# Low halves of the next weights in 32 pieces on GpSimd, gelu output rounded by ScalarE instead of VectorE

## The reference

```python
def new_gelu(x): ...                                  # tanh form
shared = new_gelu(xf @ Wfc_s + bfc_s) @ Wproj_s + bproj_s
probs = softmax(xf @ Wr); topk_p, topk_i = top_k(probs, 2)   # made to sum to 1
for e in range(8):                                    # routed experts
    h = new_gelu(xf @ Wfc[e] + bfc[e]) @ Wproj[e] + bproj[e]
    routed = routed + h * gate[:, e:e + 1]
return shared + routed
```

## Time and profile before

| what | before |
|---|---|
| median of 3 runs (lowest to highest) | 1134.1 us (1130.27 to 1138.52) |
| profiled execution, first to last instruction | 1131.3 us |
| PE busy | 982.5 us (87%) |
| DVE busy | 804.5 us (71%) |
| ACT busy | 374.5 us (33%) |
| POOL busy | 444.0 us (39%) |
| mean granted TensorE clock | 0.934 |

### The profile page before, as it was taken

How to read it: one execution, slowest core, us unless ns; L and a number is a source line. 1 busy time by engine, 2 the same in 40 slices (tenths; PEclk the granted TensorE clock), 3 DMA queues, 4 the chain that set the end, 5 groups by cost and what they waited for, 6 DMA issues and landing times.

```text
span 1131.3 us, 21584 instructions
## 1 busy us (share of the span) xinstructions
PE 982.5 (87%) x6889; PEld 910.7 (80%) x6890; DVE 804.5 (71%) x2317; ACT 374.5 (33%) x851; POOL 444.0 (39%) x496
## 2 busy tenths in 40 slices
PE   5777888999999999998888797979979799797996
PEld 3556678888888888887887797979979799797996
DVE  3467788888888888887664767676676766767664
ACT  2011234434444444433342232323323233232332
POOL 4142445332333333434222536372453624545232
PEclk9677699999999999999997898989989899898998
DMA  9200510001111110001115535354532536352232
GB/s 263 95 10 10 163 38 29 30 24 33 37 37 37 37 37 26 25 18 34 39 68 175 162 55 147 76 124 98 127 97 48 132 87 129 98 126 28 47 46 29
DMA packets 48163, 82.68 MB, mean 73 GB/s; under 512 B 6416, under 2 KB 30883, under 8 KB 48132
## 3 DMA queue, kind: packets, MB, share of 16 engines
q0 software_dynamic: 31056, 57.46, 21.4%
q1 hardware_dynamic: 17076, 24.84, 7.5%
HBM read 55.32 MB, written 26.96 MB: 73 GB/s over the span
## 4 chain that ended last, share of the span: by engine, by line
PE 48%; issue 24%; DVE 15%; POOL 9%; ACT 1%; DMA 1%; SPq 1%; POOLq 0%; DVEq 0%; ACTq 0%
PE ps_nd L660 18%; PE ps_proj L645 9%; PE ps_ri L645 5%; PE ps_proj L725 4%; PE ps_ip L645 4%; DVE rden L1254 3%; POOL out L603 2%; PE ps_nd L846 2%; POOL v_rows L497 2%; PE ps_h L833 2%; POOL h L560 1%; DVE GL L1077 1%; PE ps_t L895 1%; PE ps_h L818 1%; DVE A L1386 1%
## 5 line engine op out<-in xcount | busy, mean ns | idle before, releaser
L660 PE MATMUL ps_nd<-w2h,GH 128*128 128x256 f32 x832 | 251.9, 303 | 80.1 <-DVE GL L1077 72.4
L1511 DVE CAST GH<-g_act 128x256 fp32r<-128x256 f32 x288 | 155.7, 543 | 124.6 <-ACT g_act L953 114.3
L660 PE MATMUL ps_nd<-w2l,GH 128*128 128x256 f32 x832 | 238.5, 287 | 0.0
L660 PE MATMUL ps_nd<-w2h,GL 128*128 128x256 f32 x832 | 237.4, 285 | 0.0
L953 ACT ACTIVATE g_act<-ps_proj,fcb 128x256 f32<-128x256 f32 (+1 forms) x280 | 131.1, 469 | 319.3 <-PE ps_proj L645 315.6
L660 PEld LDWEIGHTS ps_nd<-w2h,GH 128*128 128x128 f32 x832 | 161.3, 194 | 89.5 <-DVE GL L1077 75.5
L1077 DVE TENSOR_TENSOR GL<-g_act,GH 128x256 fp32r<-128x256 f32 (+1 forms) x424 | 180.4, 433 | 10.2 <-ACT GH L989 9.9
L660 PEld LDWEIGHTS ps_nd<-w2l,GH 128*128 128x128 f32 x832 | 161.6, 194 | 0.0
L660 PEld LDWEIGHTS ps_nd<-w2h,GL 128*128 128x128 f32 x832 | 161.0, 193 | 0.0
L603 POOL DMA_INDIRECT out<-yb,rows_to x72 | 114.7, 1593 | 16.8 <-issue 13.9
L490 POOL TENSOR_TENSOR ve<-mv,eps 128x2 f32<-128x2 f32 x48 | 10.5, 219 | 280.5 <-DVE mv L1092 280.5
(11 more groups left out here) (266 smaller groups left out, 2019.1 us busy)
## 6 DMA issues: line engine op xcount, KB each, us to landing
R<-v_rows SPq DMA_DIRECT2D x37, 260.0 KB, 2.7
w1h<-fc_w POOLq DMA_DIRECT2D x9, 1024.0 KB
w2h<-pj_w POOLq DMA_DIRECT2D x9, 1024.0 KB
stage<-fc_w POOLq DMA_DIRECT2D x9, 1024.0 KB, 5.5
stage<-pj_w POOLq DMA_DIRECT2D x9, 1024.0 KB, 8.0
v_rows<-tail_rows SPq DMA_DIRECT2D x16, 260.0 KB, 3.2
x<-x SPq DMA_DIRECT2D x16, 256.0 KB, 3.6
out<-yb SPq DMA_DIRECT2D x16, 256.0 KB, 2.1
```

Source lines behind the costliest of these rows:

```text
L660: last = pe.matmul(banks[a], g[:, j, a * P:(a + 1) * P], w[i][:, j, :], start=(j == 0 and q == 0), stop=(j == HT - 1 and q == 2))
L1511: dve.tensor_copy(GH[:, j, :], g_act[:, j % G_SLOTS, :]).then_inc(gh_done, 1)
```

## The change

1. GpSimd makes the next expert's low halves with `split_fine`: 2 x 16 instructions of 128 columns instead of 4 of 1024. The arithmetic and the bytes are the same, and so are the two waits ahead and the one signal behind. The splits of the first phase stay as they are.
2. In a routed block ScalarE writes `GH`: the cast of tile j - 1 stands behind the gelu of tile j, and that of tile 7 behind the cast of tile 6. VectorE's casts are gone, and it makes `GL` of tile j where it cast tile j.

```diff
@@ experts_pool
+            def split_fine(g, i):
+                pool.wait_ge(staged, g * 32 + 32)
+                pool.wait_ge(high_loaded, g * 32 + 32)
+                for stage, high, low in ((stage1, W1H, W1L), (stage2, W2H, W2L)):
+                    for q in range(16):
+                        cols = slice(q * P, (q + 1) * P)
+                        last = pool.tensor_tensor(flat(low[i])[:, cols], flat(stage)[:, cols],
+                                                  flat(high[i])[:, cols].bitcast(F32), ALU.subtract)
+                last.then_inc(w_split, 1)
...
                 add_rows(first)
                 if prefetch:
-                    split_low(pool, g + 1, 1 - i)
+                    split_fine(g + 1, 1 - i)
                 if prefetch == 2:
                     load_stage(pool, g + 2)
@@ experts_scalar
                 for j in range(HT):
                     gelu(act, b + SBLK, i, j, fc_after)
+                    if j:
+                        high_g(act, b + SBLK, j - 1)
+                high_g(act, b + SBLK, HT - 1)
                 high_x(b + 1)
@@ experts_vector
                 for j in range(HT):
-                    dve.wait_ge(gelu_done, (b + SBLK) * HT + (j + 1))
-                    dve.tensor_copy(GH[:, j, :], g_act[:, j % G_SLOTS, :]).then_inc(gh_done, 1)
-                    if j:
-                        low_g(dve, b + SBLK, j - 1)
+                    low_g(dve, b + SBLK, j)
...
-                low_g(dve, b + SBLK, HT - 1)
                 next_x(b + 1)
```

More of the change, by code:

```diff
@@ L954, in gelu, with high_g @@
                            ACT.Gelu_apprx_tanh, bias=fcb[i][:, j:j + 1]).then_inc(gelu_done, 1)
+        def high_g(act, n, j):
+            act.wait_ge(gelu_done, n * HT + (j + 1))
+            act.copy(GH[:, j, :], g_act[:, j % G_SLOTS, :]).then_inc(gh_done, 1)
         def mixer_scalar(act):
@@ L985, in tanh_route @@
                 act.activation(rtanh[:], rdif[:], ACT.Tanh, scale=0.5).then_inc(route_act, 1)
-            def high_g(n, j):
-                act.wait_ge(gelu_done, n * HT + (j + 1))
-                act.copy(GH[:, j, :], g_act[:, j % G_SLOTS, :]).then_inc(gh_done, 1)
             def tanh_gates(n, e):
@@ L1031, in step @@
                         if j:
-                            high_g(n, j - 1)
+                            high_g(act, n, j - 1)
                     if live(t - 3) and j == 5:
```

## The result

The changed kernel takes 1157.26 us (median of 4 runs, 1155.1 to 1160.53) against 1136.31 before (4 runs): ratio 1.0191, 95% interval 1.0151 to 1.0232. It is slower, by 1.5 to 2.3%. The forecast was 1167 us with a range of 1098 to 1178. The profiled executions differ by 1153.3 - 1131.3 = 22.0 us, where 34.7 was forecast.

The account below looks back on a forecast made before the run. TensorE bounds the kernel outside splits; in seven splits it idles while GpSimd holds up VectorE. Seven times +4.5 us plus 3.2 us for blocks on 1131.3 gives 1166.0; forecast 1167 us, range 1098 to 1178.

Parts of the forecast that it names:

- the forecast's own range: Whole kernel, if VectorE stays held: 1158 to 1171 us, or 1178 counted from the slowest run; chance 0.60.
- rival 1: Routed splits: VectorE gets in between pieces, but the second block's add_rows comes late; 1089 to 1128 us, chance 0.30.
- Which instruction waits: Routed splits: with the cast gone from VectorE, the first GL behind a split's start is held instead.
- VectorE held to the end of the chain: Routed splits: the pieces keep overlapping behind the indirect DMA, so VectorE has no way in for 13.9 us.
- the sum: Seven splits at +4.5 us, 31.5, plus blocks 3.2: 34.7 us more than the profiled 1131.3, giving 1166.0 us.
- The pieces: GpSimd's split: 0.435 us per 128-column piece, 13.9 us for 32 against 9.2 before, so 4.7 us longer.
- the forecast's lower bound: GpSimd's pieces: a fixed part of 0.14 us per instruction instead of 0.17, making a split 4.0 us longer.
- the +4.5 us per split: Each routed split: 4.7 us longer chain of pieces less 0.2 us for GL; 31.5 us in seven.
- taken off 0.2: Each split: a held GL ends 0.28 us behind GpSimd, where GL after the held cast ended 0.50 behind.
- The ordinary blocks: All 36 routed blocks: tile 0's GH from ScalarE comes 0.09 us later, 3.2 us in all.
- likeliest near 1108: Whole kernel under rival 1: the likeliest time within its 1089 to 1128 us.
- the remainder of the DMA: Start of a routed split: it begins before the indirect DMA ahead ends; this overlap goes on and keeps VectorE out.

Follow-up runs that it names:

- act_cast_only: The changed kernel with the old split of 4 instructions of 1024 columns, so only ScalarE's cast stays: 1133.73 us against 1132.79, ratio 1.001.
- three_carriers_no_wait: The changed kernel with three one-element GpSimd instructions, and no wait, between the indirect DMAs and the 32 pieces: 1160.65 us, ratio 1.0235.
- drain_32: The changed kernel with a one-element GpSimd instruction, and a wait for its end, between the indirect DMAs and the 32 pieces: 1128.41 us, ratio 0.9956.
- carrier_no_wait: drain_32 without the wait; the one-element instruction stays ahead of the 32 pieces: 1126.84 us, ratio 0.9952.
- drain_4: drain_32 with the split in 4 instructions of 1024 columns instead of 32 pieces: 1111.81 us, ratio 0.9809.

## Why the prediction was right, point by point

The direction and the mechanism were right, and the loss was put too high: 34.7 us against 22.0. By the profiled executions the time, 1153.3, lies below the forecast's own range (1158 to 1171); it lies inside the stated one because that was stretched down to 1098 for rival 1.

- **Which instruction waits.** GL took the cast's place. Right: `act_cast_only` shows it by itself, 9.5 us long.
- **VectorE held to the end of the chain.** Right in its decision, with one detail wrong. In the changed kernel all seven GL were held for over 12 us, but not quite to the end: GL ended at 705.99, 0.30 behind the end of piece 30, and the last piece at 706.88. VectorE got in two pieces early, 0.9 us per split that the sum didn't have. Why is not known: over a chain the reported pieces get shorter (1056 ns the longest of the first tile, 816 the shortest of the second), but in `three_carriers_no_wait` they are shorter still, and three of the seven GL were held to the end of the chain.
- **The pieces.** 0.435 us forecast, 0.415 measured; 32 of them 13.5 us (693.37 to 706.88) instead of 13.9. The spacing is that of the forecast's lower bound (a fixed part of 0.14 us makes it 0.414). The split grew by 13.5 - 9.3 = 4.2, not 4.7.
- **The term that was mis-sized** is the +4.5 us per split, 31.5 in all. The block with the split against an ordinary one costs 24.52 - 11.97 = 12.55 now and 9.98 before: +2.6. The chain grew by 4.2. Before, the GL that TensorE needs ended 0.50 behind the chain; now it ends 0.89 before the chain's end: 1.39 less, where the sum had taken off 0.2. Together 4.24 - 1.39 = 2.85, and so it is from the DMA's end to the end of that GL: 701.54 - 691.77 = 9.77 us before, 705.99 - 693.37 = 12.62 now. TensorE's waits say nearly the same: +18.8 us in seven, 2.7 each.
- **The ordinary blocks.** 3.2 us forecast; 11.97 against 11.87 is 0.10 x 36 = 3.6. Right.
- **The sum.** 18.8 + 3.6 = 22.4 against 22.0 measured; 34.7 was forecast.
- **Rival 1.** It did not come, but its price was worked out for a state that `drain_32` then made: 1089 to 1128 us, with `rows_to` 5.0 to 10.7 us late and TensorE 3.5 to 9.2. Measured: 1128.4 in the median and 1121.6 in the profiled execution, from which that range is counted; 8.7 and 7.2. The "likeliest near 1108" was too hopeful, and not for the split: it took 15.8 us, in the lower half of the 13.9 to 19.6. But from the end of the load's issue to the landing of the added rows went 715.53 - 707.20 = 8.3 us, where 6.2 was taken from a block without a load just ahead: 2.1 more, 15 us in seven.
- **The empty start.** The reading that the remainder of the DMA keeps VectorE out is half borne out: an empty GpSimd lets it in, in every split; but how much overlap is needed to keep it out could not be told (`carrier_no_wait`, `three_carriers_no_wait`), and the hold of 59.41 came without a DMA ahead.

## What to carry to other kernels

When one engine's instructions hold up another's, cutting the long instruction into pieces helps only if the other engine is let in between them. Read that from the length of the held instruction, and not from the pieces: in `carrier_no_wait` they were reported as overlapping and VectorE got in all the same, six times of seven. What worked here every time was to let the engine run empty before the first piece. Then read the queue behind the stall: the work that stood there waits next, and here most of the gain (5.8% instead of 0.4) came only when it was put between the halves.

## What the runs showed of the hardware

- A GpSimd chain right behind an indirect DMA ran with overlapping instructions (a piece reported at up to 1.06 us with starts 0.415 apart), and VectorE was held across 30 of them, 12.5 us, in all seven splits. In chains begun on an empty GpSimd it was held for one instruction: at most 0.75 us with 128 columns, 0.99 with 256, 2.66 with 1024.
- VectorE was held across two GpSimd instructions (4.72 us) also where no DMA stood ahead and they overlapped by 0.03 us only the earlier trace rows; elsewhere, with the same overlap, it was not.
- The overlap can persist in a chain of 32 and shrinks slowly (about 7 ns a piece).
- Two-column instructions of VectorE are held as wide ones are: 2.32 us for `info_t` in `drain_4`, 0.22 where nothing holds it.
- One one-element instruction ahead of the pieces let VectorE in six times of seven, three such instructions never, each in the one profiled execution. No run here explains it.
